# The first norm's sums and scale a step ahead, the second norm's fixed scale at the split, the third score in another bank

## The reference, cut to what matters

```python
# x: (16, 375, 256); B = 16 batches, T = 374 tokens after the readout row, C = 256, E = 8 experts, D = 128
h = gelu(x[:, 1:] @ W[:C] + x[:, :1] @ W[C:] + b)

# first block: attention on cosines of the normalised rows
y = layernorm(h)                                    # (y - mean) / sqrt(var + 1e-5)
sim = (y @ y^T) / max(|y_i| * |y_j|, 1e-8)
h = h + softmax(sim) @ y + y

# second block: experts chosen by a router, causal attention over what they give
z = layernorm(h)
logits = (z / |z|) @ (sim_matrix / |sim_matrix|) - sigmoid(gates)
mask = logits > 0, or the top two experts where none is
q, k, v = sum over e of mask_e * (z @ {q,k,v}_proj[e])
a = softmax(causal(q @ k^T / sqrt(D))) @ v
h = h + sum over e of (mask * routing_weights)_e * (a @ o_proj[e])
```

## Time and profile before

| | |
|---|---|
| median of 3 runs | 727.38 us (727.03 to 729.79) |
| profiled execution | 725.99 us, of which the traced span is 724.3 |
| PE busy | 684.4 us, 94% of the span |
| DVE busy | 564.4 us, 78% |
| POOL busy | 412.1 us, 57% |
| ACT busy | 347.9 us, 48% |
| granted PE clock | 0.999 of full speed |

### The profile page before, as it was taken

How to read it: one execution, slowest core, us unless ns; L and a number is a source line. 1 busy time by engine, 2 the same in 40 slices (tenths; PEclk the granted TensorE clock), 3 DMA queues, 4 the chain that set the end, 5 groups by cost and what they waited for, 6 DMA issues and landing times.

```text
span 724.3 us, 17445 instructions
## 1 busy us (share of the span) xinstructions
PE 684.4 (94%) x4856; PEld 435.2 (60%) x4856; DVE 564.4 (78%) x1428; ACT 347.9 (48%) x768; POOL 412.1 (57%) x669
## 2 busy tenths in 40 slices
PE   9999999999898999999899999989899999989998
PEld 8888665565555555555656555555555555555555
DVE  5788788777969788796978877796978879685736
ACT  5877463633535363434446354343536344443444
POOL 7542425665656566566557566565656656562634
PEclk9999999999999999999999999999999999999999
DMA  9571243334242332423233242424223242331211
GB/s 245 143 184 45 77 94 60 92 53 96 50 108 58 55 86 47 113 52 91 56 70 84 46 101 54 97 48 108 58 55 86 47 113 49 92 59 39 49 66 36
DMA packets 128310, 57.29 MB, mean 79 GB/s; under 512 B 100264, under 2 KB 124056, under 8 KB 128152
## 3 DMA queue, kind: packets, MB, share of 16 engines
q1 hardware_dynamic: 127888, 56.60, 33.8%
q10 hardware_dynamic: 392, 0.32, 0.1%
HBM read 30.45 MB, written 9.01 MB: 54 GB/s over the span
## 4 chain that ended last, share of the span: by engine, by line
PE 55%; DVE 22%; issue 13%; POOL 5%; DVEq 1%; DMA 1%; ACT 1%; POOLq 0%; SPq 0%; ACTq 0%
PE bank L1827 46%; DVE xm L1412 8%; POOL small L662 2%; DVE region_b L1295 2%; DVE stats L1278 2%; DVE region_a L1423 2%; PE bank L1747 2%; DVE exp_hl L1433 1%; DVE h L1317 1%; PE bank L1880 1%; PE bank L1897 1%; PE bank L1893 1%; PE bank L1736 1%; PE bank L1895 1%; DVE kT L1306 1%
## 5 line engine op out<-in xcount | busy, mean ns | idle before, releaser
L1827 PE MATMUL bank<-xm,w_qkv 128*128 128x374 f16 x2304 | 410.8, 322 | 2.6 <-DVE xm L1412 2.4
L1827 PEld LDWEIGHTS bank<-xm,w_qkv 128*128 128x128 f16 x2304 | 220.9, 98 | 148.9 <-DVE xm L1412 7.4
L1412 DVE TENSOR_TENSOR xm<-xT,mask_all 128x1496 f16<-128x1496 f16 x128 | 145.8, 1144 | 7.9 <-DMA mask_all<-d_mask 7.9
L1827 PE MATMUL bank<-w_o,aoT 128*128 128x512 f16 x540 | 143.3, 379 | 7.2 <-DVE aoT L1306 7.2
L1032 ACT ACTIVATE region_c<-bank,out_w 128x256 f32<-128x256 f32 x180 | 83.3, 470 | 129.0 <-PE bank L1827 127.8
L1317 DVE SCALAR_TENSOR_TENSOR h<-bank,out_w,h 128x256 f32 (+1 forms) x180 | 86.4, 480 | 70.0 <-ACT region_c L1032 68.4
L750 POOL TENSOR_TENSOR region_c<-region_c 128x512 f32<-128x512 f32 x46 | 71.9, 1563 | 51.9 <-ACT region_c L1032 47.0
L1827 PEld LDWEIGHTS bank<-w_o,aoT 128*128 128x128 f16 x540 | 51.8, 98 | 54.9 <-issue 11.8
L789 POOL TENSOR_TENSOR exp_hl<-exp,exp_hl 128x128 f16<-128x128 f32 (+2 forms) x48 | 42.3, 882 | 28.5 <-ACT exp_hl L975 28.1
L757 POOL TENSOR_TENSOR region_c<-region_c 128x256 f32<-128x256 f32 x46 | 47.1, 1025 | 8.1 <-POOL region_c L750 7.9
L901 ACT ACTIVATE aoT<-bank 128x374 f16<-128x374 f32 x15 | 7.2, 482 | 90.4 <-PE bank L1827 90.4
(11 more groups left out here) (211 smaller groups left out, 1044.0 us busy)
## 6 DMA issues: line engine op xcount, KB each, us to landing
mask_all<-d_mask SPq DMA_DIRECT2D x32, 384.0 KB, 4.2
h<-in_x_dram SPq DMA_DIRECT2D x16, 256.0 KB, 4.9
out_dram<-h SPq DMA_DIRECT2D x31, 128.0 KB
rnorm_row<-d_rnorm SPq DMA_DIRECT2D x16, 192.0 KB, 3.9
d_v<-xinT SPq DMA_DIRECT2D x14, 192.0 KB, 4.4
xinT<-d_v SPq DMA_DIRECT2D x56, 48.0 KB, 2.3
h<-in_x_dram SPq DMA_DIRECT2D x15, 112.0 KB, 5.5
out_dram<-h SPq DMA_DIRECT2D x15, 112.0 KB
```

The lines of the kernel that those rows point to most:

```text
L1412: v.tensor_tensor(xm[:, e, :, 0:T], xT[1][:, :, :, 0:T].rearrange("p a c t -> p (a c) t"), mask_all[:, e, 0:T].unsqueeze(1).broadcast_to([ ...
L1827: last = t_.matmul(dst, left[lp], right[rp], start=(starts and k == 0), stop=(stops and k == 2), skip_group_check=True)
```

## The change

POOL: `norm_rows(0, ...)` is called for the batch after g1 and at the end of the step. With n = 1 the multiply by LN_SCALE (2^11) is dropped, and the power itself releases DVE. The later factor is applied when the second norm's rows are split. DVE: the sums of the first norm are taken for the batch after g1, behind pair 7; mask product 7 moves behind the second norm's sums. PE: `M(7)` moves behind `probs_v`, the third score goes to `turn[0]`, the bank of the logits. SP: `norms_out` moves to the front. The last trip of the loop is written out.

```diff
         def pipeline(loop_engine, step):
-            with loop_engine.Fori(3, B - 1) as i:
+            with loop_engine.Fori(3, B - 2) as i:
                 step(i, i + 1, i, i - 1, i - 2)
+            step(B - 2, B - 1, B - 2, B - 3, B - 4)
...
+        def stats_next(i):
+            return None if isinstance(i, int) and i + 2 >= B else i + 2
# SP, step
+                if g is not None and not early(m):
+                    norms_out(g)
...
                 if f is not None and not early(m):
                     second_rows_around(f)
-                if g is not None:
+                if early(m):
                     norms_out(g)
-                    if early(m):
-                        first_rows_around(g)
+                    first_rows_around(g)
                     norms_in(g)
-                    if not early(m):
-                        first_rows_around(g)
+                elif g is not None:
+                    norms_in(g)
+                    first_rows_around(g)
# POOL, norm_rows: for n == 0 as before; for n == 1
+                    g.tensor_scalar(sm[:, 0, :], v, LN_EPS, None, ALU.add).then_inc(chain, 1)
+                    pool.wait_ge(chain, per * b + 1).then_inc(s_passed, 1)
+                    g.tensor_tensor(sm[:, 1, :], sm[:, 0, :], m_half[:, :], ALU.pow).then_inc(s_scale2, 1)
+                    pool.wait_ge(s_scale2, b + 1).then_inc(s_passed, 1)
# POOL, step
+                if early(m):
+                    norm_rows(0, g1, 1.0, 1e-38)
                 if g1 is not None:
-                    norm_rows(0, g1, 1.0, 1e-38)
                     row_scales(g1)
                     low_1(g1)
                 if f is not None:
                     route_weights(f)
+                if early(m):
+                    norm_rows(0, stats_next(i), 1.0, 1e-38)
...
                     else:
                         add_tile(n, 2)
+                        if f is not None and stats_next(i) is not None:
+                            norm_rows(0, stats_next(i), 1.0, 1e-38)
# ACT, high_2; DVE, norm_apply_tile and low_2
-                a.activation(xhl[1][:, 0, :, :, :], xs[1][:, :, :, :], ACT.Copy).then_inc(s_hi2, 1)
+                a.activation(xhl[1][:, 0, :, :, :], xs[1][:, :, :, :], ACT.Copy, scale=LN_SCALE).then_inc(s_hi2, 1)
-                                moments[n][:, t, 0:1], small[n][:, 4, t:t + 1],
+                                moments[n][:, t, 0:1], small[n][:, (4, 1)[n], t:t + 1],
-                v.tensor_tensor(xhl[1][:, 1, :, :, :], xs[1][:, :, :, :], xhl[1][:, 0, :, :, :],
-                                ALU.subtract).then_inc(s_lo2, 1)
+                v.scalar_tensor_tensor(<xhl[1] low>, <xs[1]>, LN_SCALE, <xhl[1] high>,
+                                       ALU.mult, ALU.subtract).then_inc(s_lo2, 1)
# DVE, residual
-                    if m is not None and k == 2:
-                        mask_tokens(m, E - 1)
# DVE, step: the early one, then the others
+                    dve.wait_ge(s_limit1, g1 + 1)
+                    norm_stats(0, stats_next(i))
                     cosines(g1, 0)
...
-                    mask_scores(n, 2, out_bank[0])
+                    mask_scores(n, 2, turn[0])
                     mask_tokens(m, E - 3)
                     residual(f, m=m)
-                    if g1 is not None:
-                        norm_stats(0, g1)
+                    mask_tokens(m, E - 1)
                     norm_apply(1, f)
...
                     pairs(6, 8)
+                    if stats_next(i) is not None:
+                        dve.wait_ge(s_limit1, g1 + 1)
+                        norm_stats(0, stats_next(i))
                     for e in range(E - 5):
# PE, score and step
-                if i == 2:
+                if i == 2 and banks[2] is banks[0]:
                     pe.wait_ge(s_scores_out, NT * n + 1)
...
-                    score(n, 2)
+                    score(n, 2, out_bank + [turn[0]])
...
-                    M(4, 5, 6, 7)
+                    M(4, 5, 6)
                     probs_v(n)
+                    M(7)
```

More of the change, by code:

```diff
@@ L657, in norm_rows @@
                 sm, v, chain = small[n], moments[n][:, :, 1], (s_pool1, s_pool2)[n]
-                per = 5
+                per = (5, 4)[n]
                 pool.wait_ge((s_moments1, s_moments2)[n], NT * (b + 1)).then_inc(s_passed, 1)
[L660 to L664, removed]
+                if n == 0:
+                    g.tensor_scalar(sm[:, 0, :], v, LN_EPS, None, ALU.add).then_inc(chain, 1)
+                    pool.wait_ge(chain, per * b + 1).then_inc(s_passed, 1)
+                    g.tensor_tensor(sm[:, 1, :], sm[:, 0, :], m_half[:, :], ALU.pow).then_inc(chain, 1)
+                    pool.wait_ge(chain, per * b + 2).then_inc(s_passed, 1)
+                    g.tensor_scalar(sm[:, 4, :], sm[:, 1, :], LN_SCALE, None, ALU.mult).then_inc(s_scale1, 1)
+                else:
+                    g.tensor_scalar(sm[:, 0, :], v, LN_EPS, None, ALU.add).then_inc(chain, 1)
+                    pool.wait_ge(chain, per * b + 1).then_inc(s_passed, 1)
+                    g.tensor_tensor(sm[:, 1, :], sm[:, 0, :], m_half[:, :], ALU.pow).then_inc(s_scale2, 1)
+                    pool.wait_ge(s_scale2, b + 1).then_inc(s_passed, 1)
                 g.tensor_tensor(sm[:, 2, :], v, sm[:, 1, :], ALU.mult).then_inc(chain, 1)
-                pool.wait_ge(chain, per * b + 3).then_inc(s_passed, 1)
+                pool.wait_ge(chain, per * b + per - 2).then_inc(s_passed, 1)
                 g.tensor_tensor(sm[:, 3, :], sm[:, 2, :], sm[:, 1, :], ALU.mult).then_inc(chain, 1)
-                pool.wait_ge(chain, per * b + 4).then_inc(s_passed, 1)
+                pool.wait_ge(chain, per * b + per - 1).then_inc(s_passed, 1)
                 g.tensor_scalar(sm[:, 2, :], sm[:, 3, :], C * scale, floor * scale, ALU.mult, ALU.max).then_inc(chain, 1)
-                pool.wait_ge(chain, per * b + 5).then_inc(s_passed, 1)
+                pool.wait_ge(chain, per * b + per).then_inc(s_passed, 1)
                 if n == 0 and later(b):
@@ L1472, in low_2 @@
                     dve.wait_ge(s_turned2_lo, f)
-                v.tensor_tensor(xhl[1][:, 1, :, :, :], xs[1][:, :, :, :], xhl[1][:, 0, :, :, :],
-                                ALU.subtract).then_inc(s_lo2, 1)
+                v.scalar_tensor_tensor(xhl[1][:, 1, :, :, :].rearrange("p c t q -> p (c t q)"),
+                                       xs[1][:, :, :, :].rearrange("p c t q -> p (c t q)"), LN_SCALE,
+                                       xhl[1][:, 0, :, :, :].rearrange("p c t q -> p (c t q)"),
+                                       ALU.mult, ALU.subtract).then_inc(s_lo2, 1)
             def turned_low_2(f):
@@ L1918, in turn_mask, with score @@
                 last.then_inc(s_mask_turned, 1)
-            def score(n, i):
+            def score(n, i, banks=out_bank + out_bank[:1]):
                 if i == 0:
@@ L1925, in score @@
                         pe.wait_ge(s_pair_added, PAIRS * n)
-                if i == 2:
+                if i == 2 and banks[2] is banks[0]:
                     pe.wait_ge(s_scores_out, NT * n + 1)
-                split_product(out_bank[i % 2][:, 0:KEYS[i]], [qT[:, p, i * P:(i + 1) * P] for p in range(2)],
+                split_product(banks[i][:, 0:KEYS[i]], [qT[:, p, i * P:(i + 1) * P] for p in range(2)],
                               [kT[:, p, 0:KEYS[i]] for p in range(2)], True, True, s_scores_done)
```

## The result

The changed kernel took 777.49 us (median of four runs, 775.17 to 780.83), the kernel before 727.76 beside it: ratio **1.068**, 95% interval 1.063 to 1.074, **slower**. The forecast was 752 with a range of 733 to 764. The direction was right, the size forecast was half of what came: the profiled execution has a span of 773.4 against 724.3, 49.1 more where the sum said 24.5.

What follows compares the result with a forecast made beforehand. The matrix engine PE was taken as the bound, working nearly the whole span. Twelve trips at 1.80 us plus steps 1, 2 and 15 gave 24.5 us, so 750.5 profiled and, with the runs' median 1.39 higher, 752 us; range 733 to 764.

Steps and rivals of the forecast that it cites:

- 12 x 1.80 = 21.6: PE, steps 3 to 14: pair(n, 0) starts 1.80 us later in each of twelve trips, 21.6 us together.
- all four: The rivals: delay hidden, 722 (0.07); masks hold POOL, near 770 (0.12); slower landing, 769 (0.04); gaps given back, 731 to 735 (0.13).
- pair(0) = landing + 3.80: PE: after the second transpose lands, probs_v, M(7) and M(8, 9) take 3.80 us, then pair(n, 0) starts, at 282.45.
- my 6.73: POOL: from 268.87, moved norm_rows(0) and then low_probs end at 275.6, between bounds of 274.9 and 276.1.
- One sum of the forecast: ACT, then DVE, behind probs_v: heads taken after 1.23 us, 0.48 on ACT, 0.5 on DVE, done at 280.95 under M(7, 8, 9).
- steps 1, 2 and 15: Outside the twelve trips: norm_stats before step 1's cosines costs 1.4 us, M(7)'s swap 0.5 in step 2 and 0.95 in step 15.
- The scale at the split and the bank: Second norm's splits on ACT and DVE, and PE's wait before score(n, 2): both claimed to cost nothing.
- Rival (d): PE: gaps at score(n, 0) and turn_exp close when PE comes later, leaving +0.2 us a trip, 731 to 735; chance 0.13.
- Rival (b): POOL: its chain waits out one whole mask product of DVE, 0.97 us more; +3.35 a trip, near 770; chance 0.12.

Runs made afterwards that it cites:

- e2_fill: The changed kernel with 14 matrix products whose result nobody reads put on PE in front of probs_v; 759.22 us, ratio 1.044.
- e1_pool_old: The changed kernel with norm_rows(0) back behind norm_rows(1) on POOL and norms_out back in its old place on SP; 725.93 us, ratio 0.998.
- e5_delay: The kernel before with seven dependent POOL instructions on scratch, formed like norm_rows(0), behind add_tile(n, 2) in 13 steps; 786.83 us, ratio 1.083.
- e4_small: The kernel before with only the scale at the split and the third score in the logits' bank; 724.73 us, ratio 0.997.
- e3_m7_old: The changed kernel with M(7) back in front of probs_v and mask product 7 back inside the residual on DVE; 765.80 us, ratio 1.052.
- e9_idle: The changed kernel with norm_stats(0) behind norm_apply(0, g1), norm_rows(0) behind low_1(g1), M(8) ahead of probs_v and step 1 as in e7_best; 717.76 us, ratio 0.987.
- e2b_half: The changed kernel with seven unread matrix products in front of probs_v, which leaves PE a wait there; 755.82 us, ratio 1.040.
- e7_best: e1_pool_old with M(8) ahead of probs_v on PE and step 1's sums taken in DVE's idle time before weight_max; 722.87 us, ratio 0.995.
- e11_turn_only: The kernel before with one edit, turn_mask(f) one unit earlier on PE, before M(17); 733.92 us, ratio 1.007.
- e10_turn: e9_idle with turn_mask(f) one unit earlier on PE, before M(17); 705.93 us, ratio 0.970 to the kernel before.

## Why the prediction was wrong

**The step that failed: "12 x 1.80 = 21.6".** It costed `probs_v` and the three units M behind the wait at 0.95 each in every trip. The wait that the same step found, near 3 us in twelve trips, changes the rate of the work behind it. In nine of twelve trips that work took 5.15 to 6.72 instead of 3.80, together 19.7 us, and the loop is 18.6 longer than twelve full-clock trips; e2_fill, with nothing but products put in the gap, gave 19.4 of it back in the same twelve trips. Without the clock's part the same sum is 1.51 + 0.49 + 27.8 + 0.72 = 30.5, which makes 758 and lies inside the range. No rival had it: all four moved the landing of a transfer or a wait and held the price of a product fixed.

**Mis-sized in the same term: the trip at full clock.** It is +2.42, not +1.80. To `pair(n, 0)` it is 17.14 from the score against 14.95, +2.19: the formula "pair(0) = landing + 3.80" held to the hundredth, `probs_v` started 0.39 later than I had it, 0.28 of that from POOL's chain and `low_probs` (5.08 and 1.93, 7.01 together, against my 6.73; inside the bounds of 6.07 to 7.25). The other 0.23 comes behind `pair(n, 0)`: the gap at `score(n, 0)` went from 0.83 to 1.17, and PE gets 0.10 of it back at `turn_mask` (11.78 behind `pair(n, 0)`, 11.88 before). Twelve times 2.42 would be 29.0; against the twelve trips as they were before (497.77, the first of them 42.32) it is 27.8, where the forecast had 21.6. One sum of the forecast is off and nothing hangs on it: `aoT` would be there at 280.86, not 280.95.

**Right.** POOL's move is the cause, and it alone makes the kernel slow (e1_pool_old, e5_delay). PE's wait is 3.18 where 2.95 was forecast, `aoT` and mask product 7 wait no more, and steps 1, 2 and 15 cost 1.51, 0.49 and 0.72 where 1.4, 0.5 and 0.95 stood. The scale at the split and the bank cost nothing (e4_small). Rival (d), the gaps given back, did not come: the one at `score(n, 0)` grew from 0.83 to 1.17, the one at `turn_exp` stayed (10.6 and 10.5 in all).

**Rival (b)** was half right in its mechanism: mask products hold POOL up, but by 0.26 and 0.78 at two instructions of the chain, and not by a whole product on top of 4.63. The chain took 5.08 where the rows of before had 4.63 and 4.06. The 4.63 held a meeting of its own, the power of 1.30 at 281.70 beside this row of DVE, in the kernel before:

```profile
281.28 0.99 DVE L1473 TENSOR_TENSOR xhl<-region_b,xhl 128x768 f16<-128x768 f32 x1
```

The Trainium skill, SBUF — State Buffer, section Terms, has the loser at the shared ports blocked for the full instruction of the other; here the 1.02 of a three-column instruction beside a 0.93 mask product agrees, and so do `low_probs` in e3_m7_old and the first mask product in the next section.

**What was there to read.** The range left the clock out though the page of before had it as a row: it was 0.999, and no wait of PE that the earlier trace rows show is over 1.14 (the longest in its whole list is 1.2). A forecast wait of 3 us had no row of before beside it. That was the place for a bound "and if the work behind it runs at half speed": 3.80 more a trip, 12 x 3.80 = 45.6, which on top of 752 would have set the upper end near 798 rather than 764.

## What to carry to other kernels

A step moved off the path of one batch stands on the path of another: before moving it, look at which instruction of that engine comes next in the new place, who waits for its result, and by how little it is in time (here 0.85 us). A forecast wait that is longer than any in the trace of before needs a price for the work behind it as well as for itself; filling the gap with dead products tells the two apart in one run. And a gain on one engine pays only as far as the step that hands over to the others moves with it: with the early steps where their engines stand idle (e9_idle) the kernel was 1.3% faster, with `turn_mask` one unit earlier on top 3.0%, while `turn_mask` alone made it 0.7% slower.

## What the runs showed of the hardware

- **The clock.** In the changed kernel eleven waits before `probs_v` were 3.00 to 3.19 us; behind nine the clock fell, behind two it held. In e1_pool_old `probs_v` took 1.54 behind a wait of 2.14, and 1.12 behind all the shorter ones; behind the ten of 1.65 to 1.68 in e2b_half nothing fell. Waits of one length did both: 3.18 at 288.13 kept 1.00, 3.19 at 331.94 did not. What decides between them stays open; no experiment here set it. The kernel before is not free of it: of its 49 executions beside the experiments seven had a mean clock of 0.998 and took 729.56 to 731.61, and those at 1.000 took 725.42 to 729.69.
- **DVE is held up too.** The first mask product after the mask row took 0.97 before and 1.90 after, beside POOL's sum of the output products (L763); the second took 1.60 before and 1.06 after. The kernel after (DVE, then POOL), then the second product of the kernel before:

```profile
310.61 1.90 DVE L1430 TENSOR_TENSOR xm<-xT,mask_all 128x1496 f16<-128x1496 f16 x1 [0.51 <-DMA mask_all<-d_mask]
...
312.83 1.06 DVE L1430 TENSOR_TENSOR xm<-xT,mask_all 128x1496 f16<-128x1496 f16 x1
```

```profile
310.45 1.27 POOL L763 TENSOR_TENSOR region_c<-region_c 128x512 f32<-128x512 f32 x1
```

```profile
300.76 1.60 DVE L1412 TENSOR_TENSOR xm<-xT,mask_all 128x1496 f16<-128x1496 f16 x1
```

  Together the two are 0.39 longer after, and the gap at `score(n, 0)` grew by 0.34. In all kernels that have `turn_mask` in its old place the gaps at the scores of steps 4 to 14 sort by this: behind a first product of 0.94 to 1.18 the gap is 0.82 to 0.94, behind one of 1.5 to 2.1 it is 1.16 to 1.27. The kernel before has one gap of the second kind, in step 4 (2.06, gap 1.18), and e7_best has both kinds. The new place of `norm_stats` is not the cause: e1_pool_old has it and mostly a gap of 0.85, e5_delay does not have it and a gap of 1.17. No experiment set the meeting itself.
- **A 24-column instruction of 1.50 us.** One step of the route is held up beside POOL's `low_1` in the kernel before and in e11_turn_only, and is short in e10_turn, where `low_1` is done when it comes. In e7_best it is in most trips the step just ahead of that one. First e11_turn_only, then e10_turn, then e7_best:

```profile
291.32 1.50 DVE L1378 TENSOR_TENSOR lg<-lg,sig 128x24 f32<-128x24 f32 x1
```

```profile
280.85 0.18 DVE L1396 TENSOR_TENSOR lg<-lg,sig 128x24 f32<-128x24 f32 x1
```

```profile
245.35 1.67 DVE L1386 TENSOR_TENSOR lg<-lg,small 128x24 f32<-128x24 f32 x1
```

  The 1.3 us between 1.50 and 0.18 has the size of the room that let `turn_mask` move (1.28 in e9_idle, 0.05 in the kernel before). In the kernels where a step is held up (before, e1_pool_old, e4_small, e7_best, e11_turn_only) PE has no such room or waits at `turn_mask`, and e1_pool_old has DVE's sums a step ahead all the same. That speaks for POOL's `low_1` rather than for DVE's sums as what decides on the room, but no run isolated it.
